# The routing's one-hot matrices made by VectorE alone, and the third tile's gating moved to GpSimd, in a retention and mixture-of-experts layer

## What is computed

```python
xn = layernorm(x)
# branch 1, 16 heads of 16 features
q, k, v = heads(xn @ wq.T), heads(xn @ wk.T), heads(xn @ wv.T)
scores = (q @ k.T) * SCALE * gamma[h] ** (i - j) * (i >= j)
y = layernorm(merge(scores @ v)) * ln_w + ln_b
attn = (y * silu(xn @ wg.T)) @ wo.T
# branch 2, 32 experts of 192 hidden units, the best 4 for each token
logits = xn @ router_w.T + router_b
top_vals, top_idx = top_k(logits, 4)
rw = softmax(top_vals) * 1.8
routed = sum over the 4 choices of rw * (silu(xn @ gate[e].T) * (xn @ up[e].T)) @ down[e].T
shared = (silu(xn @ sg.T) * (xn @ su.T)) @ sd.T
out = x + attn + routed + shared
```

## Time and profile before

| | |
|---|---|
| median of three runs | 200.25 us (200.07 to 200.26) |
| the profiled execution's own time | 200.26 us |
| its span in the trace | 198.4 us |
| TensorE's clock granted in the span | 1.00 of full speed |
| PE busy | 190.0 us, 96% |
| DVE, POOL, ACT busy | 117.5 us, 111.8 us, 96.7 us |

### The profile page before, as it was taken

One profiled execution on the slowest core, in us unless ns is written; L12 is line 12 of the kernel. 1 busy time (PEld: TensorE's weight loads), 2 busy tenths in 40 slices (PEclk: granted clock), 3 DMA queues, 4 the chain that ended last, 5 costly groups with the idle time before them and its releaser, 6 DMA issues.

```text
span 198.4 us, 4872 instructions
## 1 busy us (share of the span) xinstructions
PE 190.0 (96%) x1734; PEld 142.7 (72%) x1734; DVE 117.5 (59%) x360; ACT 96.7 (49%) x242; POOL 111.8 (56%) x156
## 2 busy tenths in 40 slices
PE   8998999999998899899999999999999999999994
PEld 2665756778565667698888678887867877687863
DVE  3478789898897766765632532433342144426894
ACT  3146248555889342653238647734934941123500
POOL 4133057525979468777777677777877743730000
PEclk9999999999999999999999999999999999999999
DMA  4994999998000029999975634324433335229963
GB/s 133 316 374 159 332 403 421 446 444 378 7 0 3 5 56 380 384 358 366 366 288 149 223 106 140 97 90 138 123 104 98 115 91 220 79 82 292 373 262 132
DMA packets 15000, 42.33 MB, mean 213 GB/s; under 512 B 2677, under 2 KB 6138, under 8 KB 14336
## 3 DMA queue, kind: packets, MB, share of 16 engines
q1 hardware_dynamic: 11376, 33.03, 45.5%
q0 software_dynamic: 3456, 8.92, 13.3%
q10 hardware_dynamic: 144, 0.07, 0.2%
HBM read 34.66 MB, written 7.86 MB: 214 GB/s over the span
## 4 chain that ended last, share of the span: by engine, by line
PE 73%; DMA 7%; DVE 7%; issue 4%; POOL 4%; ACT 3%; SPq 0%; ACTq 0%; POOLq 0%; DVEq 0%
PE bank L1575 20%; PE bank L1591 8%; PE bank L1783 5%; PE bank L1589 5%; DMA xg_mem<-xn_rows,codes 4%; PE bank L1440 4%; PE bank L1450 3%; PE bank L1553 3%; DMA w_mem<-w_qkvg_dram 3%; PE bank L1541 3%; PE bank L1612 3%; PE bank L1515 3%; DVE w_mem L1105 2%; PE bank L1465 2%; PE bank L1817 2%
## 5 line engine op out<-in xcount | busy, mean ns | idle before, releaser
L1575 PE MATMUL bank<-xb_mem,w_mem 128*128 128x128 f32 x384 | 47.7, 276 | 0.1
L1575 PEld LDWEIGHTS bank<-xb_mem,w_mem 128*128 128x128 f32 x384 | 45.4, 192 | 0.8 <-issue 0.3
L838 POOL DMA_INDIRECT y_rows<-y_mem,codes x36 | 36.2, 1007 | 16.8 <-issue 9.4
L830 POOL DMA_INDIRECT xg_mem<-xn_rows,codes x36 | 35.4, 984 | 13.0 <-issue 9.7
L1160 DVE TENSOR_TENSOR h_mem<-h_mem,bank 128x128 f32<-128x128 f32 x32 | 9.2, 287 | 42.2 <-ACT h_mem L641 41.9
L1105 DVE TENSOR_TENSOR w_mem<-bank,w_mem 128x512 f32<-128x512 f32 x32 | 20.1, 682 | 2.9 <-PE bank L1465 2.8
L640 ACT ACTIVATE h_mem<-bank 128x128 f32<-128x128 f32 x32 | 8.9, 277 | 23.5 <-PE bank L1575 23.1
L1168 DVE COPY y_mem<-bank 128x256 f32<-128x256 f32 x36 | 15.0, 424 | 7.3 <-PE bank L1591 4.5
L653 ACT COPY w_mem<-w_mem 128x1024 f32 x16 | 16.0, 1042 | 3.2 <-PE bank L1630 2.2
L1591 PE MATMUL bank<-w_mem,h_mem 128*128 128x256 f32 x60 | 17.0, 405 | 0.0
L1440 PE MATMUL bank<-w_mem 128*128 128x128 f32 x128 | 15.9, 278 | 0.2 <-DMA w_mem<-w_qkvg_dram 0.2
(11 more groups left out here) (168 smaller groups left out, 320.7 us busy)
## 6 DMA issues: line engine op xcount, KB each, us to landing
w_mem<-w_exp_dram SPq DMA_DIRECT2D x3, 3456.0 KB, 21.6
w_mem<-w_late_dram SPq DMA_DIRECT2D x7, 1152.0 KB, 8.1
w_mem<-y_rows SPq DMA_DIRECT2D x8, 512.0 KB, 7.3
w_mem<-w_qkvg_dram SPq DMA_DIRECT2D x2, 512.0 KB, 6.3
w_mem<-decay_dram SPq DMA_DIRECT2D x2, 512.0 KB, 7.6
xn_rows<-w_mem SPq DMA_DIRECT2D x2, 512.0 KB, 3.4
xnt_rows<-w_mem SPq DMA_DIRECT2D x1, 1024.0 KB, 4.9
w_mem<-w_ovf_dram SPq DMA_DIRECT2D x16, 64.0 KB
```

The lines of the kernel that those rows point to most:

```text
L830: nc.gpsimd.indirect_dma_start(xg[:, k % RING, :], None, xn_rows, bass.IndirectOffsetOnAxis(ap=codes[:, c, 0:1], axis=0),).then_inc(tok_in ...
L838: nc.gpsimd.indirect_dma_start(y_rows, bass.IndirectOffsetOnAxis(ap=codes[:, c, 1:2], axis=0), ysb[:, k % YRING, :], None, bounds_check=RO ...
L1575: last = nc.tensor.matmul(ps_gu[j][:, m * P:(m + 1) * P], w[:, o:o + P], xbT[:, p % 2, (2 * g + j) * P:(2 * g + j + 1) * P], start=(g == 0 ...
```

## The change

`blk_code` is now made by 32 DVE instructions of 128x60, one for each a. Each compares the column numbers with that a's block number, which it reads as a [128, 1] operand, and multiplies by the constant 128 + a. One more DVE instruction (128x1920) takes the minimum of that and the row number: as every code is 128 or more and the row number below 128, this is the row number where the block is and zero elsewhere. `make_codes` subtracts 128 in place of 1. All of this stands in the list of t = 4 in the place of `one_hot_blocks`. `pos_hot` is made by 32 DVE instructions of 128x128, 16 at each of the two places where the compares with zero stood. ACT's 28 instructions and POOL's five go. The gating of tile 2 goes from DVE's list (t = 4) to POOL's (the end of t = 3, behind `spread_values(4)`), with the waits on `z_sb` that the alternation needed.

```diff
-POOL_HOT = range(5, 10)
-HOT_STEPS = {(3, "y"): 5, (4, "z"): 6, (4, "rows"): 2, (5, "tok"): 1, (5, "qk"): 2, (5, "vg"): 11}
-HOT_PARTS = 2
...
-            def code_rows():
-                act.wait_ge(blk_sb, 1)
-                nc.scalar.activation(blk_code[:, :, NB:2 * NB], blk_hot[:, :, :], ACT.Copy, scale=cst[:, C_PI:C_PI + 1]
-                                     ).then_inc(rows_sb, 1)
...
-                if t == T_RANK + 1:
-                    hot_positions()
-                if 1 <= t < NT - 2 and t != CPB - 1:
+                if 1 <= t < NT - 2:
                     gate_output(t - 1)
...
             def one_hot_positions(part):
-                a = slice(part * NA // HOT_PARTS, (part + 1) * NA // HOT_PARTS)
-                dve.wait_ge(abs_sb, a.stop - len(POOL_HOT))
-                dve.wait_ge(pool_hot_sb, len(POOL_HOT))
-                nc.vector.tensor_scalar(pos_hot[:, a, :], pos_hot[:, a, :], 0.0, None, ALU.is_equal).then_inc(pos_hot_sb, 1)
...
+                for a in range(part * NA // 2, (part + 1) * NA // 2):
+                    last = nc.vector.tensor_scalar(pos_hot[:, a, :], iota_bf[:, :], pos_f[:, a:a + 1], None, ALU.is_equal)
+                last.then_inc(pos_hot_sb, 1)
+
+            def code_blocks():
+
+                dve.wait_ge(slot_sb, 1)
+                for a in range(NA):
+                    last = nc.vector.tensor_scalar(blk_code[:, a, 0:NB], iota_bf[:, 0:NB], blk_f[:, a:a + 1], float(P + a),
+                                                   ALU.is_equal, ALU.mult)
+                step(last)
+                nc.vector.tensor_scalar(blk_code[:, :, NB:2 * NB], blk_code[:, :, 0:NB], cst[:, C_PI:C_PI + 1], None,
+                                        ALU.min).then_inc(code_sb, 1)
...
                 if t == T_RANK + 2:
-                    gate_output(CPB - 2)
-                    dve.wait_ge(pos_sb, 1)
-                    one_hot_blocks()
+                    code_blocks()
                     add_residual(t - 2)
...
                 if t == T_RANK + 3:
-                    code_blocks(1)
                     one_hot_positions(0)
...
-                if t == T_RANK + 2:
-                    code_blocks(0)
...
-                pe.wait_ge(hot_sb, 2)
-                pe.wait_ge(rows_sb, 1)
-                pe.wait_ge(pos_hot_sb, HOT_PARTS)
+                pe.wait_ge(code_sb, 1)
+                pe.wait_ge(pos_hot_sb, 2)
```

More of the change, by code:

```diff
@@ L276, in build @@
         h_mem = sb("h_mem", [P, 12 * P + 2 * I + 2 * P])
-        blk_hot = xb_mem[:, 0:NA * NB // 2].bitcast(BF16).rearrange("p (a b) -> p a b", a=NA)
         blk_code = h_mem[:, 0:NA * NB].bitcast(BF16).rearrange("p (a b) -> p a b", a=NA)
@@ L330, in build @@
         lgT_sb = sem("lgT_sb")
-        pos_sb = sem("pos_sb")
-        abs_sb = sem("abs_sb")
         pos_hot_sb = sem("pos_hot_sb")
-        pool_hot_sb = sem("pool_hot_sb")
+        slot_sb = sem("slot_sb")
+        code_sb = sem("code_sb")
         vz_sb = sem("vz_sb")
@@ L374, in build @@
         rank_sb = sem("rank_sb")
-        blk_sb = sem("blk_sb")
-        rows_sb = sem("rows_sb")
-        hot_sb = sem("hot_sb")
         inv_ps = sem("inv_ps")
@@ L704, in _ @@
                     take_output_tokens(t - 1)
-                hot_positions(t, "tok")
                 take_queries_keys(t + 1)
-                hot_positions(t, "qk")
                 if t == 0:
@@ L712, in _ @@
                     take_transposed(t - 2)
-                hot_positions(t, "z")
                 take_values_gate(t + 1)
-                hot_positions(t, "vg")
                 take_outputs(t)
@@ L718, in _ @@
                     take_features(4)
-                if t == T_RANK + 1:
-                    hot_positions(t, "y")
-                if t == T_RANK + 2:
-                    code_rows()
-                    hot_positions(t, "rows")
                 if 1 <= t < T_EXPERT:
@@ L803, in gate_output @@
                     pool.wait_ge(w_in, 48)
-                if t == CPB - 1:
-                    pool.wait_ge(z_sb, t)
                 step(nc.gpsimd.tensor_tensor(z1[:, :], yn[:, t % 2, :], lnw[:, :], ALU.mult))
@@ L809, in gate_output @@
                 nc.gpsimd.tensor_tensor(z[:, t % 2, :], z1[:, :], gate[:, t % 3, :], ALU.mult).then_inc(z_sb, 1)
[L811 to L817, removed]
             def column(b):
@@ L1054, in assign_slots @@
                 nc.vector.tensor_copy(blk_f[:, :], blk_i[:, :])
-                nc.vector.tensor_copy(pos_f[:, :], pos_i[:, :]).then_inc(pos_sb, 1)
+                nc.vector.tensor_copy(pos_f[:, :], pos_i[:, :]).then_inc(slot_sb, 1)
             def one_hot_positions(part):
-                a = slice(part * NA // HOT_PARTS, (part + 1) * NA // HOT_PARTS)
-                dve.wait_ge(abs_sb, a.stop - len(POOL_HOT))
-                dve.wait_ge(pool_hot_sb, len(POOL_HOT))
-                nc.vector.tensor_scalar(pos_hot[:, a, :], pos_hot[:, a, :], 0.0, None, ALU.is_equal).then_inc(pos_hot_sb, 1)
[L1063 to L1072, removed]
+                for a in range(part * NA // 2, (part + 1) * NA // 2):
[9 more added lines that the diff above has]
+                                        ALU.min).then_inc(code_sb, 1)
             def take_inverse():
@@ L1083, in make_codes @@
                                              ALU.is_equal, ALU.mult))
-                step(nc.vector.scalar_tensor_tensor(code_f[:, :], inv[:, 0:NB], -1.0, unused[:, :], ALU.add, ALU.add))
+                step(nc.vector.scalar_tensor_tensor(code_f[:, :], inv[:, 0:NB], -float(P), unused[:, :], ALU.add, ALU.add))
                 step(nc.vector.scalar_tensor_tensor(codes[:, 0:NB, 1], inv[:, NB:2 * NB], float(NA), code_f[:, :],
@@ L1139, in gate_output @@
                 dve.wait_ge(yn_sb, t + 1)
-                if t in (CPB - 2, NT - 3):
+                if t == NT - 3:
                     dve.wait_ge(z_sb, t)
```

## The result

The changed kernel took 206.97 us (median of four runs, 206.7 to 207.03) against 200.25 us: a ratio of 1.0335, 95% interval 1.0317 to 1.0353. It is slower by 6.7 us, where 4.1 us were forecast. The profiled execution took 207.03 us for a span of 205.2 us, 6.8 us more than before.

What follows compares the result with a forecast made beforehand. PE, busy 96% of the span, was taken as the bound. Keys' decay at 66.5, compares 2.6, stalls 1.0 and landing 0.1 put the inverse at 70.2, not 66.10: 200.26 + 4.1 = 204.4 us, range 200.3 to 206.8.

Steps and rivals of the forecast that it cites:

- The price of a compare: On DVE, start to start: 0.16 us per position compare, 0.145 us per block compare; 2.6 us for 16, 4.6 for 32.
- the stalls: At t = 4, three POOL products meet the block compares and hold DVE up by 1.5 us.
- the residual of tile 2: DVE step at t = 4, behind the block compares and minimum: starts at 56.6 in place of 53.91.
- the loss without the clock: Delay of the inverse's start, carried one for one to the end: 4.1 us.
- The second 16 position compares: At t = 5 behind the keys' decay: 2.6 us, plus 1.0 us of stalls from two POOL gating products.
- The first 16: Position compares at t = 5, ahead of residual and keys: cost nothing unless they take 1 us more.
- no stalls: Rival: dear compares, but POOL slips between them; inverse 1.5 us late, 201.8 us; chance 0.18.
- POOL starves: Rival: compares keep POOL out, so tile 2's last two products end at 56.6; 205.9 us; chance 0.07.
- PE's wait at 55.83: PE's 0.30 us wait for tile 4's decayed keys lasts until 58.45; projections end at 62.5, not 59.86.
- PE waiting at line 1488 for the keys: Sign that the forecast is right: PE waits some 2.6 us more at this line.
- the rival of slow compares: The four columns in 1.04 ns fail to come; moments 4.2 us late, inverse at 72.5, 206.7 us; chance 0.11.

Runs made afterwards that it cites:

- the positions alone: Kernel before, with only the positions made by 32 small compares on VectorE, no position steps on ACT and POOL; 204.93 us, ratio 1.0227.
- the block codes alone: Changed kernel with positions made as before (ScalarE, two compares with zero), keeping new block codes and gating move; 201.63, 203.01, 203.62 and 204.85 us.

## Why the prediction was wrong

**The direction and its cause were right.** The price of a compare, the stalls (1.5 us forecast, 6.11 - 32 x 0.145 = 1.5 measured), the residual of tile 2 (56.6; 56.72) and the loss without the clock (4.1; 4.5 us) came out as worked out. The second 16 position compares took 3.86 us, 1.3 us over 16 x 0.16, where 1.0 us of stalls was counted: all three products of tile 4's gating met them (they start at 67.46, 68.18 and 68.89), and the sum counted two. The first 16 took 3.76 us, 1.2 us over, where the sum put no stall; that cost nothing here, as the residual behind them still waited 0.18 us for PE. Of the rivals, "no stalls" and "POOL starves" fall too: a compare that met a product waited for it, and tile 2's gating ended at 51.25.

**The step that failed is the one that turned PE's waits into time.** "PE's wait at 55.83 becomes one until 58.45, and its projections, which ended at 59.86, end at 62.5" took the work behind a wait at its length of before, and the inverse likewise. Both ran at half the clock for most or all of their length: 16 projection products took 3.15 us where PE kept busy took 2.05, the inverse 3.32 us in place of 1.84. Of the first 1.1 us some 0.3 went unnoticed, since tile 3 was ready only at 62.5; PE came to it at 63.40 where 62.6 was forecast. The inverse's 1.5 us went straight to the end. Keeping PE busy gave back 2.2 us. No term of the sum and no rival had this; the earlier trace rows show the granted clock, at 1.00, and the sum took it as fixed. With the measured 2.2 us the sum is 4.1 + 2.2 = 6.3 us, 206.6 us.

**A wait was put in the wrong place.** The forecast had PE waiting at line 1488 for the keys. Most of the wait (2.29 of 2.66 us) stood two steps earlier: the key transposition waits, by the semaphore `res_sb`, for the residual of two tiles before, whose input lies in the same PSUM tile (`ps_po`). The end of the wait was right to 0.1 us (58.33; 58.45), as both steps hang on the same DVE chain. At t = 5 the same wait was missed: the run with the positions alone shows 1.59 us there, so the first 16 compares are not free once PE is ahead of them.

**The range was too narrow at the top.** Its upper end, 206.8 us, was set by the rival of slow compares (206.7), which did not come; the time lay 0.2 us over it by another mechanism.

## What to carry to other kernels

A wait of two or three microseconds on the matrix engine can cost more than itself: work behind it ran at half the clock here and made 6.7 us out of 4.5. Before work is moved onto an engine with idle time, look at what stands behind it in that engine's list and who waits for that; half of the same compares in the same place delayed nothing. Replacing one large compare by many small ones is priced by the count: fixed part and [128, 1] operand together were 0.13 of 0.145 us here.

## What was not expected

The low clock did not follow every wait alike. Behind a wait of 2.3 us it lasted some 3 us in the changed kernel and some 6 us, from 57 to 63, in the profiled execution with the block codes alone; behind 3.3 us the clock fell in the changed kernel and did not in the run with the gating back on DVE, where it had been at 0.50 from 57 to 63 us after the first wait of 2.63 us. The run with the 40 further instructions, the changed kernel up to them, had the same two waits (2.30 and 3.30 us): the first low clock lasted some 6 us, and the second set in only during the inverse, which took 2.18 us. The executions of one kernel differed too, by up to 3.2 us (201.63 to 204.85 us with the block codes alone). What decides it these runs do not show. The kernel before, whose waits there stayed below 1 us, ran at 1.00 in the windows of the earlier trace rows.

GpSimd's products and the small compares took turns: of the 32 block compares the three that met a product were held up, for 0.4 to 0.5 us each, and no product took longer than its 0.64 to 0.73 us for it. In the kernel before, beside DVE's long instructions, the same query decay took 1.64 us.
